# Nine context loads per batch, issued by ScalarE's queue instead of the sync engine's, in a gated cross-attention block

## The chip, the cores and the metric

One core of a Trainium2 chip runs the whole program. The metric is the device time of one execution in microseconds (us); what is given is the median of several runs. The engines are TensorE (PE, its weight loads PEld), VectorE (DVE), ScalarE (ACT), GpSimd (POOL) and the sync engine (SP), which issues most DMAs.

## The reference

A block of a Flamingo-like model, all in float32: layer norm of x (8 batches of 56 tokens, width 512), cross-attention to a context of 1500 rows per batch, a gated residual, and a small mixture of low-rank experts. There are 32 query heads, 8 key/value heads, each serving 4 query heads, and a head is 128 wide.

```python
q = (query @ wq).reshape(bs, sq, N_Q_HEADS, D_K).transpose((0, 2, 1, 3))
k = (key @ wk).reshape(bs, sk, N_KV_HEADS, 1, D_K)
...
v = (value @ wv).reshape(bs, sk, N_KV_HEADS, 1, D_V)
...
q = _apply_rope(q, curr_seq_pos)
k = _apply_rope(k, curr_seq_pos)
raw = jnp.einsum('bhqd,bhkd->bhqk', q, k) / scale
masked = raw + mask[:bs, None, curr_seq_pos:curr_seq_pos + sq, :sk]
attn = jax.nn.softmax(masked, axis=-1)
out = jnp.einsum('bhqk,bhkd->bhqd', attn, v)
...
x = x + jnp.tanh(g_xattn[0]) * _L0_xattn_ref(_layernorm(x, axis=-1), ctx_4096, ctx_4096, ...)
x = x + jnp.tanh(g_ffn[0]) * _L0_ffn_ref(_layernorm(x, axis=-1), L0_ffn_A, L0_ffn_B, L0_ffn_Wr)
```

## The kernel before, in words

The program has three parts, each with one instruction stream per engine, synchronised by semaphores: the query part (to about 100 us), the attention part (to about 2000 us) and the output part. To keep float32 accuracy, operands are split into a high and a low half (`..._hi`, `..._lo`), and each product is three matmuls. ScalarE makes the high halves and VectorE or GpSimd the low ones.

The attention part walks over 8 batches, and in each over 8 **head steps** g. Step g computes the scores of group g (`S`, six score chunks, into `sv_banks`), adds the mask and takes maxima on VectorE (L932, L937), exponentiates on ScalarE (L703, two halves, exp0 and exp1), transposes the probabilities on TensorE (`T0` to `T5`, L797; copied out by ScalarE L725 and VectorE L957), and weighs the values (`PV`, L814). Between these it projects the keys of the next group: `K` (L745) fills one of two `k_banks`; ScalarE copies the swapped halves out of the bank (`swap`, L659), and VectorE multiplies by the cosine table (`cos`, L870), which frees the bank. Projection `K20` is the first matmul of the third key chunk, and so the first that needs a bank back. Value projections (`V`, L761) lie between too.

The order on each engine is written out by hand in tables of words per kind of step: even, odd, "turn" (step 7, in which the next batch's context is also transposed, `C`), last and first. For an even step, such as step 0:

```python
PE_STEP["even"]:  "K00 S0 S1 K01 K02 S2 S3 K03 K10 S4 S5 K11 K12 K13 V40 K20 T0 T1 K21 V41 K22 T2 K23 PV0 V50 ..."
ACT_STEP["even"]: "exp0 swap0 exp1 swap1 Q K0 T0 T1 V4 T2 swap2 T3 T4 V5 T5 K1 K2 out"
DVE_STEP["even"]: "mask0 ... mask5 max1 cos0 sin0 rot0 cos1 T0 T1 sin1 rot1 norm T2 Q V4 inv cos2 T3 ..."
DVE_STEP["odd"]:  "mask0 mask1 mask2 max0 mask3 mask4 mask5 max1 norm cos0 sin0 inv T0 rot0 T1 T2 cos1 ..."
```

The first seven batches are one loop (`Fori`) whose body holds all eight steps; the last batch is written out behind it. `norm` is `normalise` (L917): it multiplies the attention output of the step before by `inv_b`, the reciprocal row sums broadcast to all partitions. They take a way through DRAM: VectorE forms them (`inv`, L942), SP stores them (L610), waits for the landing, and loads them back broadcast (L612). In an odd step `norm` stands ahead of `cos0`.

SP's queue in a batch (`batch`, L581): wait for the first probability transpose of step 0, then nine loads of context tiles of the next batch (`load_context`, L219, 125 x 512 floats or 250 KB each; six go to `stage` and three to `head_rows`); then per step the store of the attention rows (L579), the store of the row sums (L610), their load (L612), and the load of q for two steps later (L560). Step 7 also loads the three remaining context tiles and the mask. The function `wait_apart` (L160, L161) is a wait by itself.

`t_ready` counts the transposes that TensorE has finished, of context and of probabilities alike; `t_item(b, 0, 0, False)` is the number of those that come before the first probability transpose of batch b.

Of the kernel before, what the change touches and what calls it, by code (L numbers as in the profile page):

```python
# [35 lines left out]
STAGE_RING = STAGE_TILES + HEAD_TILES  # L36
# [109 lines left out]
def t_item(b, g, j, last):  # L146

    return b * T_ITEMS + (NT + g * PT + t_place(step_kind(g, last), "T", j))
# [7 lines left out]
def wait_apart(eng, sem, value, passed):  # L156

    eng.wait_ge(sem, value)  # L160
    eng.sem_inc(passed, 1)  # L161
# [336 lines left out]
def attention_part(nc, ctx, shared, cT, ctx_in, mask, wo, q_dram, inv_dram, attn_dram):  # L498
# [33 lines left out]
    sp_passed, dve_passed = sem("sp_passed"), sem("dve_passed")  # L532
# [10 lines left out]
    ctx_v = context_views(ctx_in)  # L543
# [13 lines left out]
    @block.sync  # L557
    def _(sp):
        def load_q(b, g):
            sp.dma_start(q_raw[:, g % 2], q_dram[g, :, bass.ds(b, 1)].rearrange("p b n -> p (b n)")).then_inc(q_loaded[g % 2], 16)  # L560


        for s in range(2):
            sp.sem_inc(attn_stored[s], 16)
        load_q(0, 0)
        sp.wait_ge(shared.q_stored[1], 16 * (HKV // 2 + 1))
        for m in range(STAGE_TILES, STAGE_RING):
            load_context(nc, sp, shared, ctx_v, 0, m)
        load_q(0, 1)
        for m in range(STAGE_RING, NT):  # L570

            sp.wait_ge(t_ready, m - STAGE_RING + 1)
            load_context(nc, sp, shared, ctx_v, 0, m)

        def store_attn(b, g):

            wait_apart(sp, attn_ready, b * HKV + (g + 1), sp_passed)
            u = (g - 1) % 2
            sp.dma_start(attn_dram[(g - 1) % HKV, :, bass.ds(b + (g > 0), 1)].rearrange("p b n -> p (b n)"), attn[:, u]).then_inc(attn_stored[u], 16)  # L579

        def batch(b, last):  # L581
            if not last:
                wait_apart(sp, t_ready, t_item(b, 0, 0, last) + 1, sp_passed)
                for m in range(STAGE_RING):
                    load_context(nc, sp, shared, ctx_v, b + 1, m)
            for g in range(HKV):
                if g == HKV - 1 and not last:
                    for m in range(STAGE_RING, NT):

                        wait_apart(sp, t_ready, c_item(b, m - STAGE_RING) + 1, sp_passed)  # L590
                        load_context(nc, sp, shared, ctx_v, b + 1, m)

                    wait_apart(sp, sv_free, RING + sv_item(b, g, SCORES), sp_passed)
                    load_mask(sp, shared, mask, b + 1)
                if g == HKV - 1 and last:


                    sp.wait_ge(k_lo, k_item(b, g, NC - 1) + 1)
                    sp.wait_ge(sv_ready, sv_item(b, g - 1, SCORES + v_fill(g - 1, VT - 1)) + 1)
                    for u in range(2):  # L600
                        sp.wait_ge(attn_stored[u], 16 * (b * steps2 + 2 + u))
                        load_attn(sp, shared, attn_dram, u, u)
                        if u == 0:
                            load_wo(sp, shared, wo, 1, 1)

                store_attn(b, g)

                wait_apart(sp, inv_ready, b * (HKV * HALVES) + (g + 1) * HALVES, sp_passed)
                with nc.allow_non_contiguous_dma("224 numbers"):
                    sp.dma_start(inv_dram[g].rearrange("h r -> r h"), inv_sum[:, :]).then_inc(inv_stored, 16)  # L610
                wait_apart(sp, inv_stored, b * (16 * HKV) + 16 * (g + 1), sp_passed)
                sp.dma_start(inv_b[:, :], inv_dram[g:g + 1].rearrange("g h r -> g (h r)").broadcast_to([P, GQ])).then_inc(inv_loaded, 16)  # L612
                if g + 2 < HKV or not last:

                    wait_apart(sp, q_lo, b * HKV + (g + 1), sp_passed)
                    load_q(b + (g + 2) // HKV, (g + 2) % HKV)
                if g == 1 and last:

                    load_wo(sp, shared, wo, 0, 0)

        sp.sem_inc(inv_loaded, 16)
        with sp.Fori(0, B - 1) as b:
            batch(b, False)
        batch(B - 1, True)
        store_attn(B, 0)

# [23 lines left out]
    @block.scalar  # L650
    def _(act):
        def k_exchange(item, s):

            act.wait_ge(k_ready, item + 1)
            if not isinstance(item, int) or item >= 2:

                act.wait_ge(k_rotated, item - 1)
            for lo in range(2):
                nc.scalar.activation(k_swap[lo * HALF:(lo + 1) * HALF, s],  # L659
                                     k_banks[(1 - lo) * HALF:(2 - lo) * HALF, s, 0:SC], ACT.Copy).then_inc(k_swapped, 1)  # L660

        def k_high(item, s, c):
            act.wait_ge(k_rotated, item + 1)
            nc.scalar.activation(k[0][:, c * SC:(c + 1) * SC], k_rot[:, s], ACT.Copy).then_inc(k_hi, 1)  # L664

        def c_high(item, s, m):
            act.wait_ge(t_ready, item + 1)
            nc.scalar.activation(cT[0][:, :, m * ST:(m + 1) * ST],
                                 t_banks[:, s, 0:DC * ST].rearrange("p (c s) -> p c s", c=DC), ACT.Copy).then_inc(t_hi, 1)

        def q_high(b, g):
            n = g % 2
            act.wait_ge(q_loaded[n], b * (16 * steps2) + 16 * (g // 2 + 1))
            nc.scalar.activation(q[0][:, :], q_raw[:, n], ACT.Copy).then_inc(q_hi, 1)

        def v_high(item, m):
            act.wait_ge(sv_ready, item + 1)
            nc.scalar.activation(v[0][:, 2 * m:2 * m + 2, :],  # L678
                                 sv_banks[0:ST, m % 2, :].rearrange("p (t n) -> p t n", t=2), ACT.Copy).then_inc(v_hi, 1)

        for what, (n, *_) in tasks(ACT_STEP["first"]):
            if what == "Q":
                q_high(0, 0)
            if what == "C":
                c_high(n, n % 2, n)
            if what == "swap":
                k_exchange(n, n % 2)
            if what == "K":
                k_high(n, n % 2, n)
            if what == "V":  # L690
                v_high(n, n)

        def step(b, g, last):
            kn = k_item(b, g + 1)
            kind = step_kind(g, last)
            for what, (n, *_) in tasks(ACT_STEP[kind]):
                s = ((g + 1) * NC + n) % 2
                if what in ("C", "T"):
                    t_bank = t_place(kind, what, n) % 2
                if what == "exp":  # L700

                    act.wait_ge(max_ready, b * (HKV * HALVES) + (g * HALVES + n + 1))
                    nc.scalar.activation(prob[n][:, :], prob[n][:, :], ACT.Exp, bias=neg_max[:, n:n + 1],  # L703
                                         accum_out=row_sum[:, n:n + 1]).then_inc(p_ready, 1)
                if what == "Q":
                    q_high(b, g + 1)
                if what == "swap":
                    k_exchange(kn + n, s)
                if what == "K":
                    k_high(kn + n, s, n)  # L710
                if what == "out":
                    act.wait_ge(o_ready, b * HKV + (g + 1))
                    nc.scalar.activation(o_lo[:, :], o_banks[:, g % 2, GQ:2 * GQ], ACT.Copy).then_inc(o_lo_copied, 1)
                if what == "wo":
                    wo_high(nc, act, shared, n, n)
                if what == "attn":
                    attn_high(nc, act, shared, n, n)
                if what == "V":
                    v_high(sv_item(b, g, SCORES + v_fill(g, n)), n)
                if what == "C":  # L720
                    c_high(c_item(b, n), t_bank, n)
                if what == "T":

                    act.wait_ge(t_ready, t_item(b, g, n, last) + 1)
                    nc.scalar.activation(pT[:, n % PT_SLOTS, :, 0, :],  # L725
                                         t_banks[0:ST, t_bank, 0:2 * GQ].rearrange("p (t n) -> p t n", t=2),
                                         ACT.Copy).then_inc(t_hi, 1)

        with act.Fori(0, B - 1) as b:
            for g in range(HKV):  # L730
                step(b, g, False)
        for g in range(HKV):
            step(B - 1, g, True)
# [595 lines left out]
```

## Time and profile before

| | |
|---|---|
| median of 3 runs | 2132.97 us (2131.81 to 2134.57) |
| the profiled execution | 2117.36 us, of which the span from first to last instruction is 2115.6 us |
| TensorE busy | 2009.1 us, 95% |
| VectorE, ScalarE, GpSimd busy | 1235.5, 1040.8, 309.9 us (58%, 49%, 15%) |
| mean granted TensorE clock | 0.976 |
| DMA moved | 95.00 MB, mean 45 GB/s |

A row of a timeline gives start, duration, engine, line, operation, what it writes and reads, the number of merged instructions and, in brackets, how long the engine was idle just before and what ended it. Times count from the start of the span. Names of matmuls: `k_banks` is a key projection, `sv_banks` scores or values, `t_banks` a transpose. DMA issues stand under SPq or ACTq, the queue of that engine's sequencer; they are not counted as busy. The granted clock is a share of full speed, so 1.00 is 2.4 GHz and 0.50 is 1.2 GHz. Batch 1 is the second; its steps 0 and 1 lie between 366 and 435 us.

### The profile page before, as it was taken

The numbers are of one execution on the slowest core, as the hardware profiler recorded it, in microseconds if no ns is written. First come the engines' busy times: TensorE is split into PE (matmuls) and PEld (weight loads), VectorE is DVE, ScalarE is ACT, GpSimd is POOL, SyncE is SP. The second block draws the span as 40 slices with busy tenths as digits, with TensorE's granted clock in tenths as the row PEclk, the third lists the DMA queues.
The fourth block names the chain that finished last, engine by engine and source line by source line (L and its number), as shares of the span: only waits on it lengthen the run. The fifth ranks groups of instructions, "written<-read, shape, count | busy, mean of one in ns | idle before, by whom it ended". The sixth has DMA issues, their size and how long they took to land. (4 is left out here: it accounts for less than half of the span.)

```text
span 2115.6 us, 36428 instructions
## 1 busy us (share of the span) xinstructions
PE 2009.1 (95%) x12372; PEld 1787.3 (84%) x12372; DVE 1235.5 (58%) x2639; ACT 1040.8 (49%) x1756; POOL 309.9 (15%) x221
## 2 busy tenths in 40 slices
PE   7998999899998999899998999899998999999898
PEld 7887998788887998788887898788887998999676
DVE  6664666466654656466654566466654656666534
ACT  5554555455544555455544555455554455555522
POOL 5410111011110111011110111011110111111200
PEclk9999999999999999999999999999999999999998
DMA  6610112201211112200211112200111112111360
GB/s 231 238 69 21 15 14 43 58 9 14 41 45 21 13 14 42 58 10 14 42 45 22 12 14 42 58 11 13 41 45 22 12 14 42 34 14 14 87 222 21
DMA packets 74962, 95.00 MB, mean 45 GB/s; under 512 B 22692, under 2 KB 49444, under 8 KB 74760
## 3 DMA queue, kind: packets, MB, share of 16 engines
q1 hardware_dynamic: 73608, 85.10, 17.4%
q10 hardware_dynamic: 1152, 7.34, 0.9%
q8 instruction: 111, 1.82, 0.4%
q14 instruction: 91, 0.75, 0.1%
HBM read 76.64 MB, written 15.77 MB: 44 GB/s over the span
## 5 line engine op out<-in xcount | busy, mean ns | idle before, releaser
L632 POOL TENSOR_TENSOR k_lo<-k_work,k_hi 128x500 fp32r<-128x500 f32 x192 | 243.8, 1283 | 1647.8 <-ACT k_hi L664 1647.8
L761 PE MATMUL sv_banks<-wv_hi,cT_hi 128*125 128x256 f32 x1536 | 444.2, 289 | 0.0
L761 PE MATMUL sv_banks<-wv_hi,cT_lo 128*125 128x256 f32 x1536 | 432.1, 281 | 0.0
L761 PE MATMUL sv_banks<-wv_lo,cT_hi 128*125 128x256 f32 x1536 | 431.9, 281 | 0.0
L725 ACT ACTIVATE pT<-t_banks 125x448 fp32r<-125x448 f32 x384 | 204.9, 542 | 384.6 <-PE t_banks L797 383.6
L957 DVE TENSOR_TENSOR pT<-t_banks,pT 125x448 fp32r<-125x448 f32 x384 | 236.3, 622 | 256.1 <-ACT pT L725 256.0
L745 PE MATMUL k_banks<-cT_hi,wk_hi 128*128 128x500 f32 x768 | 319.4, 416 | 68.9 <-DVE k_work L870 60.2
L932 DVE CUSTOM_DVE_ANT_0 prob<-sv_banks,mask_t 112x500 f32<-112x500 f32 x384 | 258.4, 678 | 187.8 <-PE sv_banks L785 181.9
L703 ACT ACTIVATE prob<-prob,neg_max 112x1500 f32<-112x1500 f32 x128 | 198.6, 1552 | 278.2 <-DVE neg_max L937 277.4
L745 PE MATMUL k_banks<-cT_hi,wk_lo 128*128 128x500 f32 x768 | 303.0, 394 | 0.0
L745 PE MATMUL k_banks<-cT_lo,wk_hi 128*128 128x500 f32 x768 | 302.9, 394 | 0.0
L761 PEld LDWEIGHTS sv_banks<-wv_hi,cT_hi 128*125 128x125 f32 x1536 | 286.3, 186 | 4.2
L761 PEld LDWEIGHTS sv_banks<-wv_hi,cT_lo 128*125 128x125 f32 x1536 | 286.8, 187 | 2.7
L761 PEld LDWEIGHTS sv_banks<-wv_lo,cT_hi 128*125 128x125 f32 x1536 | 286.3, 186 | 0.0
L814 PE MATMUL o_banks<-pT,v_hi 125*128 125x448 f32 x768 | 273.9, 389 | 3.3
L659 ACT ACTIVATE k_work<-k_banks 64x500 f32<-64x500 f32 x384 | 223.6, 582 | 13.8 <-PE k_banks L745 5.1
L797 PE MATMUL t_banks<-ident,prob 112*125 112x112 f32 x1536 | 226.1, 275 | 4.4 <-ACT prob L703 2.9
L745 PEld LDWEIGHTS k_banks<-cT_hi,wk_hi 128*128 128x128 f32 x768 | 148.8, 194 | 95.5 <-DVE k_work L870 63.1
L797 PEld LDWEIGHTS t_banks<-ident,prob 112*125 112x125 f32 x1536 | 213.2, 193 | 19.0 <-issue 3.3
L894 DVE TENSOR_TENSOR v_lo<-sv_banks,v_hi 125x512 fp32r<-125x512 f32 x192 | 132.3, 689 | 136.6 <-ACT v_hi L678 136.6
L678 ACT ACTIVATE v_hi<-sv_banks 125x512 fp32r<-125x512 f32 x192 | 114.3, 595 | 190.3 <-PE sv_banks L761 190.1
L814 PE MATMUL o_banks<-pT,v_lo 125*128 125x224 f32 x768 | 194.2, 267 | 0.0
(127 smaller groups left out, 2924.2 us busy)
## 6 DMA issues: line engine op xcount, KB each, us to landing
stage<-in_ctx_dram SPq DMA_DIRECT2D x72, 250.0 KB
attn_by_head<-attn SPq DMA_DIRECT2D x65, 112.0 KB, 1.7
wq_raw<-in_L_xattn_wq_dram SPq DMA_DIRECT2D x7, 1024.0 KB, 5.9
q_raw<-q_by_head SPq DMA_DIRECT2D x64, 112.0 KB, 4.1
inv_b<-inv_by_head SPq DMA_DIRECT2D x64, 112.0 KB, 4.4
head_rows<-in_ctx_dram SPq DMA_DIRECT2D x24, 250.0 KB
mask_t<-in_mask_BxSxS_ff_dram SPq DMA_DIRECT2D x16, 328.1 KB
stage<-in_L_xattn_wo_dram SPq DMA_DIRECT2D x4, 1024.0 KB, 6.5
```

The source lines that it names most:

```text
L632: nc.gpsimd.tensor_tensor(k[1][:, c * SC:(c + 1) * SC], k_rot[:, s], f32(k[0][:, c * SC:(c + 1) * SC]), ALU.subtract).then_inc(k_lo, 1)
L659: nc.scalar.activation(k_swap[lo * HALF:(lo + 1) * HALF, s], k_banks[(1 - lo) * HALF:(2 - lo) * HALF, s, 0:SC], ACT.Copy).then_inc(k_swapp ...
L678: nc.scalar.activation(v[0][:, 2 * m:2 * m + 2, :], sv_banks[0:ST, m % 2, :].rearrange("p (t n) -> p t n", t=2), ACT.Copy).then_inc(v_hi, 1)
L703: nc.scalar.activation(prob[n][:, :], prob[n][:, :], ACT.Exp, bias=neg_max[:, n:n + 1], accum_out=row_sum[:, n:n + 1]).then_inc(p_ready, 1)
L725: nc.scalar.activation(pT[:, n % PT_SLOTS, :, 0, :], t_banks[0:ST, t_bank, 0:2 * GQ].rearrange("p (t n) -> p t n", t=2), ACT.Copy).then_in ...
L745: mm = nc.tensor.matmul(k_banks[:, s, 0:SC], w[0][a][:, d, g * DH:(g + 1) * DH], cT[m][:, d, c * SC:(c + 1) * SC], start=(d == 0 and n == ...
L761: mm = nc.tensor.matmul(sv_banks[0:ST, m % 2, t * PAIR:(t + 1) * PAIR], cT[a][:, d, tile * ST:(tile + 1) * ST], w[1][mv][:, d, g * DH:g * ...
L797: mm = nc.tensor.transpose(t_banks[0:ST, s, col:col + ROWS], prob[h][:, (2 * j + t) * ST:(2 * j + t + 1) * ST], ident[0:ROWS, 0:ROWS])
L814: mm = nc.tensor.matmul(o_banks[:, g % 2, 0:(2 - a) * GQ], v[a][:, 2 * j + t, (g % 2) * DH:(g % 2 + 1) * DH], probs, start=(first and a == ...
L894: nc.vector.tensor_tensor(v[1][:, 2 * m:2 * m + 2, :], sv_banks[0:ST, m % 2, :].rearrange("p (t n) -> p t n", t=2), f32(v[0][:, 2 * m:2 * ...
L932: nc.vector.tensor_tensor_reduce(prob[h][:, c * SC:(c + 1) * SC], sv_banks[0:ROWS, n % 2, 0:SC], mask_t[:, c * SC:(c + 1) * SC], 1.0, LOWE ...
L957: nc.vector.tensor_tensor(pT[:, n % PT_SLOTS, :, 1, :], t_banks[0:ST, t_bank, 0:2 * GQ].rearrange("p (t n) -> p t n", t=2), f32(pT[:, n % ...
```

## The change

The nine loads and SP's wait ahead of them are taken out of SP's batch; ScalarE issues the same nine loads at the top of the loop body, behind a wait for the transposes of the batch before. Tiles, semaphores and everything else stay. The last batch has no such loads in either kernel.

```diff
         def batch(b, last):
-            if not last:
-                wait_apart(sp, t_ready, t_item(b, 0, 0, last) + 1, sp_passed)
-                for m in range(STAGE_RING):
-                    load_context(nc, sp, shared, ctx_v, b + 1, m)
             for g in range(HKV):
...
         with act.Fori(0, B - 1) as b:
+
+            act.wait_ge(t_ready, t_item(b, 0, 0, False))
+            for m in range(STAGE_RING):
+                load_context(nc, act, shared, ctx_v, b + 1, m)
             for g in range(HKV):
                 step(b, g, False)
```

Behind the first place line numbers fall by four (L703 is L699 in the changed kernel), and from the second on they are as before.

On ScalarE, at the head of the loop body, this stood before (prob is written by the two exponentials, k_work by the swap; ISA and REGISTER_ALU are register work):

```order
L729 UNCONDITIONAL_BRANCH
L729 ISA
L703 ACT_TABLE_LOAD
L703 ACTIVATE prob,row_sum<-prob,neg_max 112x1500 [waits max_ready]
L654 ISA
L657 REGISTER_ALU [waits k_ready]
L659 ACTIVATE k_work<-k_banks 64x500 [waits k_rotated]
```

and this stands there now:

```order
L725 UNCONDITIONAL_BRANCH
L725 ISA
L219 ISA [waits t_ready]
L219 DMA stage<-in_ctx_dram 125x512
L219 ISA
L219 DMA stage<-in_ctx_dram 125x512
...
L219 DMA head_rows<-in_ctx_dram 125x512
L698 ISA
L699 ACT_TABLE_LOAD
L699 ACTIVATE prob,row_sum<-prob,neg_max 112x1500 [waits max_ready]
```

Nine issues, each with register work ahead of it, now come ahead of the table load and of both exponentials.

On SP, at the head of its loop body, the difference is:

```order
-L622 UNCONDITIONAL_BRANCH
-L622 ISA
-L219 ISA [waits t_ready]
-L219 DMA stage<-in_ctx_dram 125x512
...
-L219 DMA head_rows<-in_ctx_dram 125x512
-L160 ISA
+L618 UNCONDITIONAL_BRANCH
+L618 ISA
 L579 ISA [waits attn_ready]
 L579 DMA attn_by_head<-attn 128x224
```

The attention store of step 0, and with it everything behind it, now comes first in the batch.

## Rows read from the trace of the kernel before

**Rows 1.** Waits of the engines: who waited for whom, us in total, times, longest.

```profile
DVE attn L917 <- DMA inv_b<-inv_by_head: 66.6, 8, 9.7
...
PE k_banks L745 <- DVE k_work L870: 60.2, 7, 9.1
```

**Rows 2.** Timeline of VectorE, batch 1, steps 0 and 1: start, us, instruction.

```profile
384.95 0.21 DVE L942 RECIPROCAL inv_sum<-row_sum 112x1 f32<-112x1 f32 x2
...
409.46 0.39 DVE L917 TENSOR_TENSOR attn<-o_sum,inv_b 128x224 f32<-128x224 f32 x1 [9.68 <-DMA inv_b<-inv_by_head]
```

**Rows 3.** Timeline of TensorE, batch 1, step 1.

```profile
401.03 0.39 PE L745 MATMUL k_banks<-cT_lo,wk_hi 128*128 128x500 f32 x1
410.50 0.79 PE L745 MATMUL k_banks<-cT_hi,wk_hi 128*128 128x500 f32 x1 [9.08 <-DVE k_work L870]
```

**Rows 4.** Timeline of SP's queue, batch 1, steps 0 and 1: every DMA issue but two.

```profile
379.49 3.63 SPq L219 DMA_DIRECT2D stage<-in_ctx_dram  x6
383.31 6.18 SPq L219 DMA_DIRECT2D head_rows<-in_ctx_dram  x3
389.85 1.47 SPq L579 DMA_DIRECT2D attn_by_head<-attn  x1
391.52 0.34 SPq L610 DMA_DIRECT2D inv_by_head<-inv_sum  x1
404.67 0.34 SPq L612 DMA_DIRECT2D inv_b<-inv_by_head  x1
...
411.26 0.33 SPq L610 DMA_DIRECT2D inv_by_head<-inv_sum  x1
417.43 0.32 SPq L612 DMA_DIRECT2D inv_b<-inv_by_head  x1
```

**Rows 5.** Timeline of VectorE, batch 1: L963 closes steps 0, 1, 2, 3.

```profile
392.30 0.39 DVE L963 TENSOR_TENSOR o_sum<-o_banks,o_lo 128x224 f32<-128x224 f32 x1 [1.45 <-ACT o_lo L713]
...
434.37 0.39 DVE L963 TENSOR_TENSOR o_sum<-o_banks,o_lo 128x224 f32<-128x224 f32 x1 [0.33 <-ACT o_lo L713]
...
459.05 0.39 DVE L963 TENSOR_TENSOR o_sum<-o_banks,o_lo 128x224 f32<-128x224 f32 x1 [1.45 <-ACT o_lo L713]
...
489.07 0.39 DVE L963 TENSOR_TENSOR o_sum<-o_banks,o_lo 128x224 f32<-128x224 f32 x1 [0.33 <-ACT o_lo L713]
```

**Rows 6.** Stretches of batch 1: length, engines' busy us, granted clock, DMA share, GB/s.

```profile
384.00:390.00 6.00, 6.00 (x50) 5.92 (x49) 4.76 (x11) 2.83 (x6) 0.00 (x0) 1.00 0.33 128
...
410.50:416.20 5.70, 5.70 (x18) 4.92 (x19) 1.87 (x5) 0.54 (x1) 0.00 (x0) 0.50 0.09 20
```

**Rows 7.** Timeline of ScalarE, batch 1: the head of the loop body.

```profile
368.15 1.28 ACT L703 ACT_TABLE_LOAD   x1 [2.30 <-issue]
372.92 1.55 ACT L703 ACTIVATE prob<-prob,neg_max 112x1500 f32<-112x1500 f32 x1 [3.49 <-DVE neg_max L937]
...
374.58 1.19 ACT L659 ACTIVATE k_work<-k_banks 64x500 f32<-64x500 f32 x2
375.80 1.55 ACT L703 ACTIVATE prob<-prob,neg_max 112x1500 f32<-112x1500 f32 x1
```

**Rows 8.** Timeline of ScalarE, batch 5: the head of the loop body.

```profile
1317.67 1.28 ACT L703 ACT_TABLE_LOAD   x1 [2.23 <-issue]
1324.39 1.55 ACT L703 ACTIVATE prob<-prob,neg_max 112x1500 f32<-112x1500 f32 x1 [5.44 <-DVE neg_max L937]
```

**Rows 9.** DMA issues by line, min/median/max ns: batch 1's first six loads; ScalarE's stores.

```profile
L219 SPq DMA_DIRECT2D stage<-in_ctx_dram x6: 263/292/1033, 379.5 to 382.1; - x6
...
L405 ACTq DMA_DIRECT2D q_by_head<-q_rot x4: 343/352/388, 30.9 to 90.4; - x4
```

**Rows 10.** Timeline of TensorE, batch 1: transposes T0 and T1 of step 0.

```profile
378.65 1.02 PE L797 MATMUL t_banks<-ident,prob 112*125 112x112 f32 x8
```

**Rows 11.** Timeline of TensorE, batch 5: the head of the loop body.

```profile
1316.84 0.49 PE L745 MATMUL k_banks<-cT_hi,wk_hi 128*128 128x500 f32 x1 [1.79 <-issue]
```

**Rows 12.** The stretch behind it, columns as in rows 6.

```profile
1317.40:1320.80 3.40, 3.40 (x10) 2.55 (x9) 0.80 (x3) 1.28 (x1) 0.00 (x0) 0.50 0.04 10
```

## The prediction, made before the changed kernel was run

> **What bounds the kernel now.** TensorE is busy 95% of the span, so I looked for the places where it is not. The list of waits comes first [rows 1]: two entries belong together. TensorE stands still seven times, 60.2 us in all and at most 9.1 us, before a key projection that waits for VectorE's L870, and VectorE stands still eight times, 66.6 us in all, before the normalisation L917, until the reciprocal row sums (inv_b) have landed. Seven is the number of batches that load the next batch. The timelines of batch 1 show that it is one stall per batch, in head step 1: VectorE starts L917 at 409.46 after 9.68 us of waiting, so it was ready at 399.8 [rows 2], and TensorE, whose bank VectorE was to free, is idle from 401.4 to 410.50 [rows 3].
>
> Why inv_b is late is read from the sync queue [rows 4]. At 379.49, when the first probability transpose of step 0 is done, it begins nine context loads. Six issues take 3.63 us, the last three 6.18 us, since the queue takes no more until earlier ones have drained: 10.0 us for nine. Only at 389.85 does it store the attention rows and at 391.52 the row sums, behind 2.3 MB of context. That store lets the next issue go 13 us later (404.67); in step 1 the same pair lies 6.2 us apart (411.26 and 417.43). inv_b then takes another 4.8 us.
>
> What the stall is worth: L963 closes a head step. Step 1 lasts 434.37 - 392.30 = 42.1 us, step 3, which has the same work, 489.07 - 459.05 = 30.0 [rows 5]. Of the 12.05 us between them 9.08 are the gap and 3.0 are slow matmuls after it: for 5.7 us TensorE's granted clock is 0.50 [rows 6], its 1.2 GHz level. Over the seven batches the gap is 8.6 us on average and, reading all seven such steps in the same way, the slow stretch adds about 2.5: about 77 us lie in this place.
>
> **What the change removes.** SP loses nine DMA issues and their wait. Its first work in a batch is then the attention store of step 0, as soon as L917 of step 0 has run, the row-sum store, inv_b and the next q load. Nothing of it stands behind context on its own queue. Will inv_b be in time? In step 0 VectorE forms the reciprocals at 384.95 now [rows 2]; with the delay that I find below, at about 391. The store takes 6.2 us, inv_b 4.8, so it lands at about 403, while L917 of step 1 is due at 399.8 plus the same delay of 5 to 6 plus some slow matmuls: 405 or later. It waits for nothing, and the context has drained by then: 2.3 MB at the 128 GB/s of [rows 6] are 18 us from 369, until 387. So the stall in step 1 goes whole: 60 us of gap, and its slow stretch.
>
> **What it adds.** ScalarE issues the nine loads at the head of the loop body, ahead of everything else. The wait for t_ready is met: it asks for the transposes of the batch before, which TensorE finished long ago. Behind the issues stand, in order, the table load, exp0, the swap of key chunk 0, exp1, the second swap, and the first copy of transposed probabilities. TensorE waits for the first swap through VectorE (projection K20) and for exp1 directly (transpose T0).
>
> How much room is there? In batch 1 the table load starts at 368.15 and exp0 at 372.92, held by the row maximum [rows 7]: 4.77 us. In batch 5 it is 6.72 [rows 8]; the other five lie at 4.6 to 5.5, the mean of the seven is 5.1. In this room must go: 0.2 us to the first issue, the nine issues, 0.1 us, and the table load of 1.28 us.
>
> The nine issues are the disputed price. No row shows a burst on ScalarE's queue; its eight issues in the query part stand alone and take 0.35 us each, as single ones on SP do [rows 9]. The bounds: 0.52 us each if nothing holds them up (3.63 less the slow sixth one of 1.03, over five) [rows 4, 9], 4.7 in all; 2.06 us each, 6.18 over three, if each is held up from the first, 18.5 in all. I take 10.0: the same nine transfers, started on an empty queue, took this on SP, and the single issues cost alike.
>
> So exp0 starts 0.2 + 10.0 + 0.1 + 1.28 = 11.6 us after the loop head, 6.8 us late in batch 1, 11.6 - 5.1 = 6.5 on average. From exp0 to the end of exp1 ScalarE has no slack (372.92, 374.58, 375.80 [rows 7]), so exp1 ends 6.5 us later. TensorE has some: exp1 ends at 377.35 and T0 starts at 378.65 [rows 10], 1.3 us. TensorE's new gap, partly ahead of K20 and partly ahead of T0, is 6.5 - 1.3 = 5.2 us per batch. ScalarE's copies behind it come 1 us later relative to TensorE, but it idles between them and catches up.
>
> Does the clock fall after the new gap as after the old? At the head of batch 5 a gap of 1.8 us was followed by a stretch at 0.50 [rows 11, 12], and all seven old gaps of 8.4 to 9.1 by one; 5.2 us lies between, so I let the slow stretch cost what it costs now, and it cancels. If it did not come, 7 x 2.5 = 17 us more would be saved. The other edits are free: nine issues fewer on SP, which waits most of its time, and the same bytes; instruction fetches and the table's own transfers that meet the context cost ScalarE some tenths.
>
> **Sum.** Per batch 8.6 saved, 5.2 paid: 3.4 us, times seven 24 us. The profiled execution took 2117.4 us (span 2115.6); the three timed runs have a median of 2133.0, 15.6 above it. I take the difference off the median: **2109 us**. With the issues at 9.5 to 11 us, the gap off by half a microsecond, and the slow stretch between none and the present one, this case reaches from 2086 to 2120.
>
> **Rivals.**
> - *The issues on ScalarE are not held up.* Then 0.2 + 4.7 + 0.1 + 1.28 = 6.3 us, 1.2 late, and the 1.3 us of slack cover it: no gap at all, 77 us saved, about 2056. For it: single issues are cheap on both queues [rows 9]. Against: SP was held up from the sixth load on with nothing else in its queue [rows 4]. Chance 0.11. On this the Trainium skill, page "DMA: Bandwidth & Descriptors", section "Issuing engines are not separate DMA queues", says that initiating on several engines saves only sequencer time, "usually small relative to the DMA itself"; by that, this rival would be the rule. The row speaks otherwise: 10.0 us of issuing for some 18 us of transfer.
> - *ScalarE's queue takes fewer loads ahead*, and the mechanism that moved becomes dearer: slower. At the bound of 18.5 us exp0 comes 15.0 us late, the gap is 13.7 instead of 8.6, and the time 2133 + 7 x 5.1 = 2169. It decides from 13.4 us of issuing on: there the gap in step 0 is as long as the one removed from step 1. For it: no burst on this queue was seen, and ScalarE, unlike SP, has dependent work behind each issue. Chance 0.12.
> - *The loads are issued in 12.8 to 14 us*, because instruction fetch and table load compete with the context on the same DMA engines: the stall has moved and nothing is left of the gain, within 4 us of 2133. Chance 0.07. That the loads don't in fact start earlier, because the wait binds, belongs here; it has no chance worth naming.
>
> **How the numbers follow.** The forecast has 0.70: faster by over 0.2% (4.3 us, about what a measurement can tell) nearly throughout. A hundredth of it goes to slower, for an effect that I don't see. With the first rival faster comes to 0.80; same 0.07; slower 0.13. Cases of the forecast and the third rival hold 0.77, so the range goes from 2086 a little beyond 2133, to 2136.
>
> **What would show it.** In the profile after: L917 has almost no wait on inv_b; the projection's wait on L870 in step 1 is gone and one of about 5 us stands in step 0, ahead of K20 or T0; step 1 lasts 30 us, step 0 about 34 instead of 26.4; ScalarE issues nine loads over some 10 us, and exp0 is held by this and not by the row maximum. I would be wrong if the nine issues took under 6 us or over 13, or if L917 of step 1 still waited.

## The result and the profile after

The changed kernel takes 2097.8 us (median of 4 runs, 2096.8 to 2099.5), the kernel before 2132.4 (4 runs): a ratio of 0.984, 95% interval 0.982 to 0.986. The profiled executions differ by less, 2117.4 against 2096.8 us; that gap between the two comparisons is taken up below.

The waits of the engines in the changed kernel (us in total, times, longest), against [rows 1]:

```profile
ACT L699 <- issue: 87.8, 7, 13.8
...
PE k_banks L745 <- DVE k_work L870: 38.1, 7, 6.6
...
DVE attn L917 <- DMA inv_b<-inv_by_head: 3.9, 1, 3.9
```

L917's seven waits in step 1 are gone; the one that is left stands at the end of the last batch. TensorE still stands still seven times, but for 38.1 us instead of 60.2, and ScalarE now has idle time, up to 13.8 us, that ends with no semaphore: most of it goes into issuing. The timeline of ScalarE and its queue at the head of batch 1, against [rows 7]:

```profile
358.25 0.36 ACT L709 ACTIVATE o_lo<-o_banks 128x224 f32<-128x224 f32 x1 [0.15 <-PE o_banks L814]
361.05 4.91 ACTq L219 DMA_DIRECT2D stage<-in_ctx_dram  x6
366.11 6.06 ACTq L219 DMA_DIRECT2D head_rows<-in_ctx_dram  x3
372.27 1.28 ACT L699 ACT_TABLE_LOAD   x1 [13.67 <-issue]
373.57 1.54 ACT L699 ACTIVATE prob<-prob,neg_max 112x1500 f32<-112x1500 f32 x1
```

Nine issues take 11.1 us here. exp0 follows the table load with no wait for the row maximum. TensorE's timeline, step 0 of batch 1, against [rows 3, 10]:

```profile
377.27 0.78 PE L745 MATMUL k_banks<-cT_hi,wk_hi 128*128 128x500 f32 x1 [6.58 <-DVE k_work L870]
378.69 1.86 PE L797 MATMUL t_banks<-ident,prob 112*125 112x112 f32 x8
```

The first row is K20, which waited for swap0 and the bank; T0 and T1 come behind it at half speed. A stretch of this slow part, with columns as in [rows 6]:

```profile
377.30:382.90 5.60, 5.60 (x20) 5.08 (x21) 4.04 (x7) 3.75 (x8) 1.26 (x1) 0.50 0.24 90
```

SP's queue in the same batch, against [rows 4]:

```profile
383.71 0.34 SPq L579 DMA_DIRECT2D attn_by_head<-attn  x1
387.26 0.33 SPq L606 DMA_DIRECT2D inv_by_head<-inv_sum  x1
394.47 0.32 SPq L608 DMA_DIRECT2D inv_b<-inv_by_head  x1
```

The row-sum store now lets inv_b go after 7.2 us instead of 13. The ends of step 7 of the batch before and of steps 0 and 1, against [rows 5]:

```profile
358.64 0.39 DVE L963 TENSOR_TENSOR o_sum<-o_banks,o_lo 128x224 f32<-128x224 f32 x1 [0.33 <-ACT o_lo L709]
...
394.31 0.39 DVE L963 TENSOR_TENSOR o_sum<-o_banks,o_lo 128x224 f32<-128x224 f32 x1 [1.45 <-ACT o_lo L709]
...
424.32 0.39 DVE L963 TENSOR_TENSOR o_sum<-o_banks,o_lo 128x224 f32<-128x224 f32 x1 [0.33 <-ACT o_lo L709]
```

Step 1 lasts 30.0 us, the undisturbed length, in all seven batches. Step 0 lasts 35.7 here, and 33.6 to 35.7 in batches 1 to 6, where it was 26.2 to 28.3. The stall has moved one step ahead and become shorter.

### The profile page after: what moved, and what is told of

Same layout as the page of the kernel before. It is cut to its first block and busy times, and to the rows that moved or that the text cites. A ratio compares the mean times of both kernels' runs of the same rounds, so it can differ in the third digit from the quotient of the medians.

```text
span 2095.1 us, 36423 instructions
## 1 busy us (share of the span) xinstructions
PE 2009.8 (96%) x12372; PEld 1790.1 (85%) x12372; DVE 1235.5 (59%) x2639; ACT 1042.1 (50%) x1756; POOL 310.5 (15%) x221
## 5 line engine op out<-in xcount | busy, mean ns | idle before, releaser
L745 PE MATMUL k_banks<-cT_hi,wk_hi 128*128 128x500 f32 x768 | 316.7, 412 | 47.2 <-DVE k_work L870 38.1
L699 ACT ACTIVATE prob<-prob,neg_max 112x1500 f32<-112x1500 f32 x128 | 198.5, 1551 | 251.4 <-DVE neg_max L937 250.5
```

What stands on the lines that cost most here:

```text
L745: mm = nc.tensor.matmul(k_banks[:, s, 0:SC], w[0][a][:, d, g * DH:(g + 1) * DH], cT[m][:, d, c * SC:(c + 1) * SC], start=(d == 0 and n == ...
```

## The experiments

The change does two things at once: it gives the loads to another queue, and it starts them earlier, since ScalarE waits for the batch before only, and SP waited for T0. The first experiments take them apart. Ratios are to the kernel before, run on the same chip in the same hour, with 95% intervals.

| kernel | us | ratio |
|---|---|---|
| changed kernel: ScalarE, early | 2097.8 | 0.984 (0.982 to 0.986) |
| SP, early | 2057.0 | 0.967 (0.965 to 0.968) |
| ScalarE, late | 2100.1 | 0.987 (0.985 to 0.988) |
| five on ScalarE early, four on SP | 2040.9 | 0.959 (0.957 to 0.960) |
| seven on ScalarE early, two on SP | 2053.6 | 0.967 (0.966 to 0.969) |
| SP, behind step 1 | 2042.3 | 0.959 (0.958 to 0.961) |
| SP, behind the row maximum | 2075.0 | 0.978 (0.976 to 0.980) |
| nine loads left out | 2038.8 | 0.960 (0.959 to 0.962) |
| kernel before, again | 2123.7 | 1.000 (0.999 to 1.002) |
| kernel before, 128 rows a load | 2039.1 | 0.964 (0.962 to 0.965) |
| changed kernel, 128 rows a load | 2042.3 | 0.965 (0.963 to 0.967) |

**SP, early.** The kernel before, with the changed kernel's wait:

```diff
-                wait_apart(sp, t_ready, t_item(b, 0, 0, last) + 1, sp_passed)
+                wait_apart(sp, t_ready, t_item(b, 0, 0, last), sp_passed)
```

> The nine loads stay on SP, only their wait is the changed kernel's (the transposes of the batch before, not T0 of this one). Theory A (what costs is when the loads go: behind T0 they hold the row-sum chain up; ScalarE's issuing is a pure cost): SP issues them over 10 us from about 362 to 372 in batch 1, the row-sum store at 385 finds the context drained, L917 of step 1 doesn't wait, exp0 isn't held up, no gap in step 0 or 1: about 2055 us. Theory B (what helped is that the row sums no longer share a queue with the context): the stall in step 1 stays wholly or in large part, time 2110 to 2133.

2057.0 us. L917 of step 1 doesn't wait, step 1 lasts 30.0 us: theory A. Starting earlier is enough to remove the stall; giving the same early loads to ScalarE costs 37 to 41 us against leaving them on SP (37 by the ratios 0.984 and 0.967, 41 by the times, which come from different sessions). One thing wasn't expected: steps 0 of batches 1 to 6 last 28.6 to 29.5 us, not 26.3. Six such differences of 2.8 us are 17, nearly the whole distance to the floor of 2039 us found below. That I had expected 2055 and came so close was luck: my base was too high by about as much. SP, VectorE and ScalarE around the jump to the head of the loop:

```profile
348.17 3.83 SPq L219 DMA_DIRECT2D stage<-in_ctx_dram  x6
352.18 6.17 SPq L219 DMA_DIRECT2D head_rows<-in_ctx_dram  x3
...
355.29 0.39 DVE L963 TENSOR_TENSOR o_sum<-o_banks,o_lo 128x224 f32<-128x224 f32 x1 [0.33 <-ACT o_lo L713]
361.76 0.68 DVE L932 CUSTOM_DVE_ANT_0 prob<-sv_banks,mask_t 112x500 f32<-112x500 f32 x1 [6.07 <-issue]
...
360.39 1.28 ACT L703 ACT_TABLE_LOAD   x1 [5.12 <-issue]
```

The loads are in flight while all engines jump back. ScalarE stands 5.1 us ahead of the table load, 2.3 in [rows 7]; VectorE 6.1 us ahead of its first mask operation, with no semaphore to wait for. Two packets of the instruction queue start at 354.5 and 358.3, 3.8 us apart; at the same jump of the kernel before they start at 364.2 and 367.5, 3.3 apart.

**ScalarE, late.** The loads stand in ScalarE's program behind its first copy of transposed probabilities:

```diff
+                    if g == 0 and n == 0 and not last:
+                        for m in range(STAGE_RING):
+                            load_context(nc, act, shared, ctx_v, b + 1, m)
```

> The nine loads are issued by ScalarE, but behind its first copy of transposed probabilities in step 0, so as late as in the kernel before. Both theories: ScalarE is held for about 10 us, and TensorE waits 6 to 8 us in step 0 for the copies behind. Theory B: the row-sum store lands in about 6.5 us though context is in flight, and L917 of step 1 doesn't wait: 2115 to 2125. Theory A, strictly (the context's traffic itself delays the small store, whichever queue): the store takes 10 us or more, L917 of step 1 waits again some 5 us: 2150 or more.

2100.1 us, below both forecasts. The gap in step 0 was 4.2 to 6.1 us, 5.3 on average, and not 6 to 8. Over seven batches that is some 12 of the 15 to 25 us by which theory B's forecast was missed. The timelines of ScalarE, TensorE and SP's queue in batch 1:

```profile
377.46 4.11 ACTq L219 DMA_DIRECT2D stage<-in_ctx_dram  x5
381.72 6.26 ACTq L219 DMA_DIRECT2D head_rows<-in_ctx_dram  x3
388.09 0.54 ACT L721 ACTIVATE pT<-t_banks 125x448 fp32r<-125x448 f32 x1 [10.48 <-issue]
...
389.34 1.18 PE L796 MATMUL t_banks<-ident,prob 112*125 112x112 f32 x4 [6.11 <-DVE pT L956]
...
392.55 0.33 SPq L606 DMA_DIRECT2D inv_by_head<-inv_sum  x1
401.43 0.32 SPq L608 DMA_DIRECT2D inv_b<-inv_by_head  x1
```

With context in flight on the other queue the row-sum store lands after 8.8 to 10.5 us (seven batches); behind context on its own queue it took 12.2 to 13.1; with nothing in flight 6.5 to 7.2 (changed kernel). That looks as if a queue of its own gave back half of the delay, but the store is also issued later here: 13.6 to 15.5 us after the first load, against 11.9 to 12.8 in the kernel before. Counted from the first load, inv_b is issued after 24.0 to 25.0 us (mean 24.4) here and after 24.8 to 25.4 (mean 25.1) there. So the other queue gives back about 0.6 us, and the traffic keeps the rest.

L917 of step 1 waits at most 1.4 us all the same, for another reason: ScalarE's hold-up has made L917 itself late. In batch 1 it is ready 28.8 us after the first load, in the kernel before 20.3. Theory B hardly holds, and of theory A the part that the traffic delays the store whichever its queue does; its wait of 5 us didn't come because L917 was late itself. The Trainium skill, page "DMA: Bandwidth & Descriptors", section "Queues, rings and completion order", has each DMA engine take turns between queues packet by packet. From that I would expect a small store on its own queue to pass between the packets of the context. The 0.6 us measured here show little of it, and why stays open.

**Five on ScalarE, four on SP.** `range(5)` at the top of ScalarE's loop body, `range(5, STAGE_RING)` on SP behind the q load of step 0.

> ScalarE issues only the first five loads at the top of the batch (those that are not held up), SP the other four behind the q load of step 0. Theory (the price on ScalarE is the hold-up from the sixth load on): five issues take 2.3 to 3 us, exp0 again waits for the row maximum, the 5 us gap in step 0 goes, step 1 keeps none: about 2055 us. Rival (each issue costs ScalarE much the same, or the head of the loop suffers by any burst): a gap of 2 to 3 us stays in step 0, 2075 to 2085.

2040.9 us, 14 below what I had expected, while the gaps went as expected: the base was too high (see the account of the prediction). ScalarE, batch 1:

```profile
356.27 2.82 ACTq L219 DMA_DIRECT2D stage<-in_ctx_dram  x5
359.19 1.28 ACT L703 ACT_TABLE_LOAD   x1 [5.50 <-issue]
360.58 1.55 ACT L703 ACTIVATE prob<-prob,neg_max 112x1500 f32<-112x1500 f32 x1
```

No gap is left in step 0, so the price lay in the issues from the sixth on. The five took 2.6 to 3.0 us in six batches, and 4.4 in batch 5, where the third issue alone took 2.3.

**Seven on ScalarE, two on SP.** The same with seven.

> ScalarE issues seven loads at the top, SP the last two behind the q load of step 0. Theory (room of 5.1 us, slack of 1.3 us, hold-up from the sixth load on): seven issues take about 6 us, exp0 is about 2.5 us late, TensorE's gap in step 0 is about 1.2 us and mostly without a slow stretch: 2045 to 2058. Rival (a threshold: once held up at all, the whole gap comes): 2075 or more.

2053.6 us. Seven issues took 4.9 to 7.0 us; TensorE's list of waits shows what is left of the gap:

```profile
PE k_banks L749 <- DVE k_work L874: 7.6, 5, 2.5
```

The price follows the time that ScalarE is held, roughly as the prediction has it: seven issues in 7.0 us, with 1.6 us around them, a room of 5.1 and a slack of 1.3, make a gap of 2.2 us. Four batches had such bursts. In three of them the gap was 2.0 to 2.5 us, in the fourth only 0.4, though step 0 grew as much there.

**SP, behind step 1.** All nine on SP behind the q load of step 1, where nothing is needed from SP for 30 us.

> All nine loads on SP behind the q load of step 1, where the row-sum chain of step 1 is done and the next begins some 30 us later. If the two stalls are all that the loads cost, neither is left: steps 0 and 1 last about 26.3 and 30.0 us, and the time is about 2055 us. Rival (the loads cost through their traffic wherever they stand, or the stall moves to L917 of step 2 or 3): a gap shows in steps 2 or 3, and the time stays above 2075.

2042.3 us, again 13 below the expected 2055, with steps 0 and 1 undisturbed. The nine issues took 11.6 to 12.9 us there and nobody waited.

**SP, behind the row maximum.** The early wait, and a second one:

```diff
+                wait_apart(sp, max_ready, b * (HKV * HALVES) + 1, sp_passed)
```

> All nine loads on SP, behind the row maximum of step 0: 7 us before the kernel before, 11 us later than with the early wait, and so behind every engine's jump to the head of the loop. Theory (with the early wait the instruction fetch of that jump was held up by context traffic, which made step 0 29.2 instead of 26.3 us): step 0 is back at about 26.3 us, the row-sum store of 385 lands at about 394, inv_b at about 398.5, just in time: 2041 to 2048 us. Rival (the 2.9 us come from nine loads on SP or their traffic beside step 0's work): step 0 stays at 29 us, 2055 us. If the row sums come late by 1 to 3 us, step 1 shows it: 2050 to 2065.

2075.0 us. Step 0 is back at 26.2 to 26.6 us (28.3 in batch 2; the kernel before has one such step too): the 2.8 us came with loads in flight during the jump, not with SP's loads as such. But step 1 kept a gap of 2.3 to 3.6 us, and the time missed even the last of my ranges. The traced execution took 2068.1 us, the shortest of the four; where the others spend up to 10 us more no trace shows. SP's queue, batch 1:

```profile
365.16 3.82 SPq L219 DMA_DIRECT2D stage<-in_ctx_dram  x6
369.17 5.99 SPq L219 DMA_DIRECT2D head_rows<-in_ctx_dram  x3
375.51 1.48 SPq L579 DMA_DIRECT2D attn_by_head<-attn  x1
377.29 0.34 SPq L611 DMA_DIRECT2D inv_by_head<-inv_sum  x1
390.10 0.34 SPq L613 DMA_DIRECT2D inv_b<-inv_by_head  x1
```

From the first load to inv_b's issue it is 24.9 us here, and 25.2 in [rows 4], with the store issued 12 us after the first load in both. The context keeps the DMA engines busy until 387.9 (share 0.2 to 0.4), 22.7 us after the first load, and inv_b goes 2.2 us later: the small store doesn't land before the context ahead of it, and for the context the 18 us of the prediction are too short here. I had expected the landing 4 us too early.

**Nine loads left out.** `sp.sem_inc(stage_loaded[m], 16)` in place of each load, so that later batches compute on old context.

> The nine loads of each batch are left out (the semaphores are counted up by SP instead, so that batches 1 to 7 work on context that is mostly batch 0's); the three loads in step 7 stay. It shows the floor: what remains of the loads' cost in a placement without stalls. Theory: nothing remains, 2040 to 2043, as with five loads on ScalarE and four on SP. Rival: the traffic itself costs something wherever it stands, 2030 or less here.

2038.8 us: the floor. The two best placements lie 2 to 4 us above it (on other chips), so loads that nobody waits behind cost next to nothing.

**The kernel before, again.**

> The kernel before, unchanged, for a second trace. Its profiled execution took 2117 us and all other executions 2126 to 2137, while the changed kernel's lie within 3 us of each other. Theory: the difference sits in the stall that the change removes (longer gaps ahead of K20 in step 1, or a longer slow stretch behind them), so steps 1 take more than the 40.4 to 42.1 us of the first trace and all other steps the same. Rival: it is spread over the program or sits at its ends (query or output part), and would not go with the stall.

Its trace spans 2122.3 us, 6.7 more than the first one:

```profile
DVE attn L917 <- DMA inv_b<-inv_by_head: 73.1, 8, 10.8
...
PE k_banks L745 <- DVE k_work L870: 66.1, 7, 10.2
```

The gaps are about 6 us longer, and the seven steps 1 take 292.8 us together instead of 287.6, 5.2 of the 6.7; every other step but a few steps 0 is the same within 0.1. So the kernel before varies with its stall, for which DMA latency counts three times in a row (context, store, load). The executions above 2130 us have left no trace of their steps, and that their excess sits there too is an inference.

**128 rows a load.** What remained was why nine loads take so long. A load has 125 rows, and during them the DMA share is 0.33 of 16 engines [rows 6], about five. Both kernels, with a helper that loads three rows more, into partitions that nothing reads:

```diff
+        self.c_slots_128 = [(self.stage if n < STAGE_TILES else head_tiles)[0:P, n % STAGE_TILES, :] for n in range(STAGE_RING)]
...
+def load_context_128(nc, sp, shared, ctx_in, b, m):
+    sp.dma_start(shared.c_slots_128[m], ctx_in[bass.ds(b, 1), m * ST:m * ST + P].rearrange("b p d -> p (b d)")).then_inc(shared.stage_loaded[m], 16)
```

> The kernel before, but each of the nine loads brings 128 rows (three more than needed, into partitions that nothing reads) instead of 125. Theory C (a load of 125 rows runs on 5 of the 16 DMA engines, as the DMA share of 0.33 says, and a load of 128 rows on all 16; both prices, the stall behind the loads and the hold-up of their issues, come from that): the nine issues take about 4.5 us, the context is in at some 8 us after the first issue, the row-sum store of 385 lands in about 7 us, L917 of step 1 hardly waits: 2040 to 2050. Rival (the queue itself takes some 2 us a load, whatever engines it uses): the issues take 10 us again and the stall stays, 2110 to 2130.

> The changed kernel with 128 rows a load. Theory C: ScalarE is through with nine issues in 4.5 to 5 us, exp0 is 1 to 1.5 us late, and TensorE has no gap in step 0, or less than 1 us: 2040 to 2050. Rival (the queue itself takes some 2 us a load): ScalarE is held for 10 us and TensorE waits 5 us again, 2095 to 2100.

2039.1 and 2042.3 us. The order of the kernel before, untouched, with 2.4% more bytes in its loads, is at the floor. One part of the expectation failed: the row-sum store took 8.8 to 10.8 us and not 7. It is now issued 5.8 us after the first load, with context still ahead of it, and L917 of step 1 waited once, for 0.7 us. SP's queue, then a stretch of the transfer (columns as in [rows 6]), of the kernel before with 128 rows:

```profile
367.09 3.08 SPq L225 DMA_DIRECT2D stage<-in_ctx_dram  x6
370.35 1.36 SPq L225 DMA_DIRECT2D head_rows<-in_ctx_dram  x3
372.07 0.35 SPq L585 DMA_DIRECT2D attn_by_head<-attn  x1
372.85 0.34 SPq L616 DMA_DIRECT2D inv_by_head<-inv_sum  x1
381.69 0.33 SPq L618 DMA_DIRECT2D inv_b<-inv_by_head  x1
```

```profile
368.00:374.00 6.00, 6.00 (x45) 5.72 (x44) 4.59 (x11) 2.65 (x6) 0.53 (x1) 1.00 0.93 283
```

Nine issues take 4.6 us here, each 0.33, and 4.6 to 5.0 in all batches: hardly one is held up. The DMA share is 0.93 and the rate 283 GB/s, where it was 0.33 and 128. ScalarE in the changed kernel with 128 rows:

```profile
356.99 3.24 ACTq L225 DMA_DIRECT2D stage<-in_ctx_dram  x6
360.39 1.33 ACTq L225 DMA_DIRECT2D head_rows<-in_ctx_dram  x3
361.81 1.28 ACT L705 ACT_TABLE_LOAD   x1 [7.37 <-issue]
```

It is through in 4.7 us, and TensorE waits 0.7 us for these swaps in the whole run. Theory C holds on both queues. The Trainium skill, page "DMA: Bandwidth & Descriptors", section "Why a DMA increments its semaphore by 16 and not by 1", says that a DMA is split over the largest number of engines, up to 16, that divides the slowest dimension on both of its sides, and names 16 for 128 partitions; for 125 rows that rule gives 5, by my estimate. The trace agrees: a DMA share of 0.33 is 5.3 engines of 16, and 0.93 is 14.9.

## Why the prediction was right, and where it was off

- **The stall and its cause**: right. L917 waited for inv_b behind the context loads; with them gone from SP and started earlier it doesn't. The runs add that the earlier start does this, and the other queue next to nothing (0.6 us).
- **The price of nine issues on ScalarE**, the disputed one, taken as 10.0 us from SP's burst: measured 8.4 to 11.1, mean 10.3. Single issues at 0.35 us would have misled; the first rival (no hold-up, 2056 us) falls, and so do the second (a shorter queue, 2169) and the third (12.8 to 14 us of issuing).
- **The new gap**: 5.2 us a batch forecast, 38.1 / 7 = 5.4 measured, ahead of K20 as described. It ran from 2.5 us in batch 0 to 6.6 in batch 1, a wider scatter than I gave it.
- **The slow stretch**: comes after the new gap as well (granted clock 0.50 over 5.6 us in batch 1), as assumed. Steps 0 of batches 1 to 6 grew by 50.4 us together, 35.6 of them gaps; the rest is 2.5 us a batch, what the old stretch cost.
- **inv_b in time**: right: expected at about 403 in the old frame with the need at 405 or later; measured landed 3.5 us ahead of L917 in batch 1. The context took 21 us and not 18 from its first load, which didn't matter.
- **The sum**: 24 us forecast. Between the two profiled executions the spans differ by 20.5, between the medians by 34.6. The step that failed is the last: "I take the difference off the median". The sum began from an execution of 2117.4 us, 15.6 below the median, and took its stall of 8.6 us a batch as typical. The second trace shows the stall longer by about 6 us over the seven batches, so the removed term was smaller than usual. The runs without either stall show the right base: they took 2039 to 2042 us; 2117.4 less the 77 us of the stall is 2040, and 2133 less 77 is 2056. Each of them repeats within 2 or 3 us, and they agree across three sessions in which the kernel before moved from 2129 to 2116. Taken off the profiled execution, from which the 8.6 us were read, the same 24 us give 2093 for the 2097.8 measured. Part of the 34.6 stays unexplained by any trace, and the kernel before itself came out at 2132, 2129, 2123 and 2116 us in four sessions, so the ratio of 0.984 belongs to the first of them.
- **What I didn't see**: that all but a fraction of the gain was the earlier wait, and that SP could have had it alone (2057); and that the DMA share of 0.33 in a row I quoted was the cause of both prices.

## What to carry to other kernels

Moving a burst of DMA issues to a compute engine moves its hold-up too: price it by a burst of the same transfers, not by single issues, and compare it with the engine's room at that place. Before moving transfers about, look at the DMA share while they run: a load that keeps a third of the engines busy has a shape problem, and here three rows more in each load were worth more than the whole move. A small transfer on which a chain hangs belongs ahead of a bulk one, or far behind it; another queue alone gave it 0.6 us here. A stall that varies from execution to execution is taken off the execution in which it was measured. And a change of place that also changes a wait should be tested one part at a time.

## What the runs showed of the hardware that I had not expected

- 125 rows against 128 in one load: 128 against 283 GB/s. In SP's bursts the seventh to ninth issues took 1.7 to 2.6 us each with 125 rows, and 0.33 to 0.63 with 128.
- A jump to the head of the loop during the bulk loads cost ScalarE 5.1 instead of 2.3 us, and about 2.8 us of step 0.
- A small store of 0.9 KB took 6.5 to 7.2 us alone, 8.8 to 10.5 beside bulk traffic of another queue, 12.2 to 13.1 behind bulk on its own. Counted from the bulk's first load the two differ by 0.6 us.
- In 10 of ScalarE's 14 bursts of nine (changed kernel and late loads) one issue took 3.1 to 4.0 us; SP's longest in the kernel before was 2.6. The sums are alike, and the cause stays open.
